# Last attention of a twelve-stage network: the first pass over a sequence taken in two halves, the preparation of its rows in two parts

## The reference

```python
def _L3_attn_ref(x, ln_g, ln_b, Wq, bq, Wk, bk, Wv, bv):
    H = 16
    xn = (x - mu) * jax.lax.rsqrt(var + EPS) * ln_g + ln_b
    q = (xn @ Wq + bq).reshape(B, T, H, D // H)      # k and v likewise
    scale = 1.0 / math.sqrt(D // H)
    attn = jnp.einsum('bnhd,bmhd->bnmh', q, k) * scale
    w = jax.nn.softmax(attn, axis=2)
    y = jnp.einsum('bnmh,bmhd->bnhd', w, v).reshape(B, T, D)
    return y
```

## Time and profile before

| what | value |
|---|---|
| median of three runs | 2432.96 us (2432.85 to 2443.46) |
| the profiled execution | 2443.27 us |
| its span, first to last instruction | 2441.4 us |
| mean granted TensorE clock | 0.865 |
| TensorE busy | 1996.0 us (82%) |
| VectorE busy | 1398.0 us (57%) |
| ScalarE busy | 960.0 us (39%) |
| GpSimd busy | 139.1 us (6%) |
| the stage of the change | about 2064 to 2345 us of the span |

### The profile page before, as it was taken

One profiled execution on the slowest core, in us unless ns is written; L12 is line 12 of the kernel. 1 busy time (PEld: TensorE's weight loads), 2 busy tenths in 40 slices (PEclk: granted clock), 3 DMA queues, 4 the chain that ended last, 5 costly groups with the idle time before them and its releaser, 6 DMA issues. The chain is left out here.

```text
span 2441.4 us, 38225 instructions
## 1 busy us (share of the span) xinstructions
PE 1996.0 (82%) x13180; PEld 1561.6 (64%) x13180; DVE 1398.0 (57%) x3614; ACT 960.0 (39%) x2141; POOL 139.1 (6%) x195
## 2 busy tenths in 40 slices
PE   3588778669967884997999899999799975888775
PEld 2355455358953223997999678787699963555543
DVE  6645455666668997666222256667522247555547
ACT  1345444332223321223444355555344444333344
POOL 1100000110001002000000000000000000000000
PEclk9779788769989995998999999999899987666668
DMA  5000000000000001000000044444100000000000
GB/s 139 31 1 1 1 1 1 31 16 1 0 1 0 1 0 50 1 0 1 1 0 0 20 136 130 129 134 129 32 1 0 0 0 0 1 1 0 0 1 17
DMA packets 47459, 61.63 MB, mean 25 GB/s; under 512 B 7126, under 2 KB 44726, under 8 KB 46744
## 3 DMA queue, kind: packets, MB, share of 16 engines
q1 hardware_dynamic: 47356, 60.31, 8.0%
HBM read 34.08 MB, written 26.21 MB: 25 GB/s over the span
## 5 line engine op out<-in xcount | busy, mean ns | idle before, releaser
L760 ACT ACTIVATE m2a_hid<-psum,m_b 128x256 f32<-128x256 f32 x256 | 100.5, 475 | 114.6 <-PE psum L55 114.5
L760 ACT ACTIVATE m2b_hid<-psum,m_b 128x256 f32<-128x256 f32 x256 | 100.5, 475 | 114.2 <-PE psum L55 114.2
L745 PE MATMUL psum<-m_w,m2a_hid 128*128 128x128 f32 x1024 | 126.2, 277 | 0.0
L745 PE MATMUL psum<-m_w,m2b_hid 128*128 128x128 f32 x1024 | 126.2, 277 | 0.0
L778 DVE SCALAR_TENSOR_TENSOR m2a_acc<-psum,m2a_gates,m2a_acc 128x128 f32<-128x128 f32 x128 | 39.0, 347 | 148.4 <-PE psum L745 148.4
L778 DVE SCALAR_TENSOR_TENSOR m2b_acc<-psum,m2b_gates,m2b_acc 128x128 f32<-128x128 f32 x128 | 39.0, 347 | 148.1 <-PE psum L745 148.1
L745 PEld LDWEIGHTS psum<-m_w,m2a_hid 128*128 128x128 f32 x1024 | 122.1, 194 | 0.6
L745 PEld LDWEIGHTS psum<-m_w,m2b_hid 128*128 128x128 f32 x1024 | 122.1, 194 | 0.6
L2150 ACT ACTIVATE a_p<-a_p,a_nmax 128x256 f32<-128x256 f32 x128 | 64.0, 500 | 143.0 <-DVE a_nmax L2174 143.0
L1881 DVE TENSOR_REDUCE a_nmax<-psum 128x2 f32<-128x512 f32 x128 | 82.9, 687 | 49.5 <-PE psum L1722 49.4
L1115 DVE TENSOR_TENSOR_SCAN a1s_clamped<-a1s_clamp_coef,a1s_bounds 128x1024 f32<-128x1024 f32 x48 | 108.7, 2267 | 0.0
(11 more groups left out here) (625 smaller groups left out, 5509.4 us busy)
## 6 DMA issues: line engine op xcount, KB each, us to landing
a_scratch<-a_pos SPq DMA_DIRECT2D x64, 384.0 KB, 2.7
a_shifted<-a_scratch SPq DMA_DIRECT2D x64, 256.0 KB, 3.1
m_w<-in_m_w SPq DMA_DIRECT2D x1, 2048.0 KB
arena<-in_m_w SPq DMA_DIRECT2D x1, 2048.0 KB, 10.4
arena<-in_m_up SPq DMA_DIRECT2D x1, 1792.0 KB, 7.0
arena<-in_m_pick SPq DMA_DIRECT2D x2, 896.0 KB, 4.5
a_w<-in_a_w SPq DMA_DIRECT2D x1, 1536.0 KB, 7.8
out<-X SPq DMA_DIRECT2D x1, 1024.0 KB, 5.0
```

Source lines behind the costliest of these rows:

```text
L745: last = nc.tensor.matmul(ps_y(e % 2)[:, t * D:(t + 1) * D], hid[:, e % 2, c * SEQ + t * P:c * SEQ + (t + 1) * P], m.m2_w2[:, e, c, :], st ...
L760: last = nc.scalar.activation(hid[:, e % 2, c * SEQ:(c + 1) * SEQ], ps_up(e % 2)[:, c * SEQ:(c + 1) * SEQ], ACT.Gelu, bias=m.m2_b1[:, e * ...
```

## The change

The stack `st` gets a second buffer, chosen by `u`. The taking of the rows (`start_c`, now the one addition) and their splitting (`start_e`, new) are parted, with a new semaphore `rows_taken` between the addition and the second shifted turn, which writes the same bank. `turn_stack` becomes `turn_keys` (rounds 0 and 1) and `turn_queries` (rounds 2 and 3 and v). In a unit heads 8 to 15 of the sequence's own first pass stand among score groups 1 to 3, and heads 0 to 7 of the next sequence's among groups 5 to 7; the second shift stands ahead of group 4. The norm's beginning is taken two units ahead, so all engines use `threaded_two_ahead`: units 0, then a loop of two rounds over the units 1 and 2, then units 5, 6 and 7 written out. ScalarE's `unit` keeps its calls, with `move_shifted(u, n, 1)` behind group 3 and `move_values(u, n, 1)` ahead of group 5.

```diff
-        st = sbr("st", [P, PAIR, 2, HEADS, 4 * HD])
+        st = sbr("st", [P, 2, PAIR, 2, HEADS, 4 * HD])
...
             def start_a(u, n):                       # TensorE
                 if not isinstance(n, int) or n:
-                    pe.wait_ge(shift_moved, 2 * n)
+                    pe.wait_ge(shift_moved, 2 * n - 1)
...
+            def turn_queries(u, n):
+                if not isinstance(n, int) or n:
+                    pe.wait_ge(shift_moved, 2 * n)
+                turn_heads(ps_stack(2), u, 0, 0).then_inc(turned, 1)
+                pe.wait_ge(moved, 4 * n + 1)
+                turn_heads(ps_stack(3), u, 0, 1).then_inc(turned, 1)
                 pe.wait_ge(moved, 4 * n + 2)
...
+            def turn_shifted(u, n, half, next_rows):
                 pe.wait_ge(shift_ready, 2 * n + half + 1)
+                if next_rows:
+                    pe.wait_ge(rows_taken, n + 2)
+                turn_heads(ps_x, u, 0, half).then_inc(shift_turned, 1)
...
-                for h in range(HEADS):
+                for h in range(8):
                     plain_scores(0, 0, h)
+                turn_shifted(0, 0, 0, False)
                 scores(0, 0, 0)
...
+            def unit(u, n, prev, next, next2):       # TensorE
+                scores(u, n, 1)
+                if prev:
+                    values(1 - u, n - 1, 3)
+                if next:
+                    start_a(1 - u, n + 1)
+                for h in (8, 9):
+                    plain_scores(u, n, h)
+                if next:
+                    start_b(1 - u, n + 1)
+                for h in (10, 11):
+                    plain_scores(u, n, h)
+                scores(u, n, 2)
+                if prev:
+                    turn_back(1 - u, n - 1, 3)
+                for h in (12, 13):
+                    plain_scores(u, n, h)
+                scores(u, n, 3)
+                for h in (14, 15):
+                    plain_scores(u, n, h)
+                values(u, n, 0)
+                turn_shifted(u, n, 1, next)
+                turn_back(u, n, 0)
+                scores(u, n, 4)
+                if next:
+                    turn_keys(1 - u, n + 1)
+                    turn_queries(1 - u, n + 1)
+                scores(u, n, 5)
+                values(u, n, 1)
+                if next:
+                    for h in range(4):
+                        plain_scores(1 - u, n + 1, h)
+                scores(u, n, 6)
+                turn_back(u, n, 1)
+                if next:
+                    for h in range(4, 8):
+                        plain_scores(1 - u, n + 1, h)
+                scores(u, n, 7)
+                values(u, n, 2)
+                if next:
+                    turn_shifted(1 - u, n + 1, 0, False)
+                turn_back(u, n, 2)
+                if next:
+                    scores(1 - u, n + 1, 0)
...
+            def unit(u, n, prev, next, next2):       # VectorE
+                if next:
+                    start_b(1 - u, n + 1)
+                for h in range(8, 12):
+                    maxima(u, n, h)
+                if next:
+                    start_c(1 - u, n + 1)
+                if prev:
+                    normalise(1 - u, n - 1, 3)
+                for h in range(12, 16):
+                    maxima(u, n, h)
+                shift(u, n, 1)
+                if next:
+                    start_e(1 - u, n + 1)
+                if prev:
+                    end_a(1 - u, n - 1)
+                normalise(u, n, 0)
+                if next:
+                    start_d(1 - u, n + 1)
+                    for h in range(4):
+                        maxima(1 - u, n + 1, h)
+                if prev:
+                    end_b(1 - u, n - 1)
+                normalise(u, n, 1)
+                if next:
+                    for h in range(4, 8):
+                        maxima(1 - u, n + 1, h)
+                    shift(1 - u, n + 1, 0)
+                if next2:
+                    start_a(u, n + 2)
+                normalise(u, n, 2)
...
-            threaded(dve, first, unit, tail)
+            threaded_two_ahead(dve, first, unit, tail)
```

More of the change, by code:

```diff
@@ L1692, in start_b, with turn_heads @@
                 last.then_inc(qk_ready, 1)
-            def turn_heads(out, a, half):
+            def turn_heads(out, u, a, half):
                 for j in range(2):
@@ L1697, in turn_heads, with turn_keys @@
                         heads = slice(8 * half + 4 * j, 8 * half + 4 * j + 4)
-                        last = nc.tensor.transpose(out[:, j, t * P:(t + 1) * P], st[:, t, a, heads, :].rearrange("p h f -> p (h f)").bitcast(F32),
+                        last = nc.tensor.transpose(out[:, j, t * P:(t + 1) * P], st[:, u, t, a, heads, :].rearrange("p h f -> p (h f)").bitcast(F32),
                                                    m.ident[:, :])
                 return last
-            def turn_stack(u, n):
+            def turn_keys(u, n):
                 pe.wait_ge(st_ready, n + 1)
[L1704 to L1707, removed]
+                for r in range(2):
+                    turn_heads(ps_stack(r), u, 1, r).then_inc(turned, 1)
+            def turn_queries(u, n):
[4 more added lines that the diff above has]
+                turn_heads(ps_stack(3), u, 0, 1).then_inc(turned, 1)
                 pe.wait_ge(moved, 4 * n + 2)
@@ L1761, in first @@
                 start_b(0, 0)
-                turn_stack(0, 0)
-                for h in range(HEADS):
+                turn_keys(0, 0)
+                turn_queries(0, 0)
+                for h in range(8):
                     plain_scores(0, 0, h)
-                turn_shifted(0, 0, 0)
+                turn_shifted(0, 0, 0, False)
                 scores(0, 0, 0)
[L1768 to L1794, removed]
@@ L1798, in tail @@
                 turn_back(u, n, 3)
-            threaded(pe, first, unit, tail)
+            threaded_two_ahead(pe, first, unit, tail)
         @block.scalar
@@ L1807, in start_b, with move_stack @@
                 nc.scalar.activation(xT[:, :], ps_x[:, 0, :], ACT.Identity, bias=m.a3_ln_b[:, 0:1], scale=m.a3_ln_g[:, 0:1]).then_inc(xT_ready, 1)
-            def move_stack(u, n):
-                for r in range(4):
+            def move_stack(u, n, turns):
+                for r in turns:
                     act.wait_ge(turned, 4 * n + r + 1)
@@ L1829, in first @@
                 start_b(0, 0)
-                move_stack(0, 0)
+                move_stack(0, 0, range(4))
                 move_shifted(0, 0, 0)
[L1833 to L1848, removed]
+            def unit(u, n, prev, next, next2):
+                exps(n, 0)
+                if prev:
+                    move_values(1 - u, n - 1, 3)
+                if next:
+                    start_b(1 - u, n + 1)
+                exps(n, 1)
+                exps(n, 2)
+                exps(n, 3)
+                move_values(u, n, 0)
+                move_shifted(u, n, 1)
+                exps(n, 4)
+                if next:
+                    move_stack(1 - u, n + 1, range(4))
+                move_values(u, n, 1)
+                exps(n, 5)
+                exps(n, 6)
+                exps(n, 7)
+                move_values(u, n, 2)
+                if next:
+                    move_shifted(1 - u, n + 1, 0)
+            threaded_two_ahead(act, first, unit, lambda u, n: move_values(u, n, 3))
         @block.vector
@@ L1886, in shift @@
                 low = nmax[:, heads, :].rearrange("p h t -> p t h")
[L1887 removed]
+                nc.vector.tensor_copy(st[:, u, :, 0, heads, 3 * HD], low)
                 nc.vector.drain()
[L1889 removed]
+                nc.vector.tensor_tensor(st[:, u, :, 0, heads, 3 * HD + 1], low, st[:, u, :, 0, heads, 3 * HD].bitcast(F32), ALU.subtract).then_inc(shift_ready, 1)
             def normalise(u, n, j):
@@ L1916, in first @@
                 start_b(0, 0)
+                start_a(1, 1)
                 start_c(0, 0)
+                start_e(0, 0)
                 start_d(0, 0)
-                for h in range(HEADS):
+                for h in range(8):
                     maxima(0, 0, h)
[L1921 to L1949, removed]
```

34 lines of the change are left out of this document (22 added, 12 removed).

## The result

The changed kernel takes 2415.13 us (median of four runs, 2411.7 to 2418.23) against 2436.99 us of the kernel before on the same chip: ratio 0.9897, 95% interval 0.9876 to 0.9918. It is faster, by 21.9 us of medians where 14.2 were forecast. Its profiled execution took 2418.23 us, 25.0 less than that of the kernel before.

The account below looks back on a forecast made before the run. No engine is full; TensorE and VectorE waiting for each other, and the clock, set a period. Periods -13.3, start -4.4 and last unit +3.5 sum to -14.2 us, from median 2432.96 to 2418.8; range 2406 to 2435.

Parts of the forecast that it names:

- start: Stage up to its first scores: first shifted turn 5.0 us earlier, second stack's memsets +0.6, together -4.4 us.
- periods: Seven stretches from one unit's first scores to the next's: each from 32.04 to 30.14 us, together -13.3 us.
- last unit: Unit after the seven periods: gets eight more products and maxima at low clock, forecast +3.5 us.
- the walk of a unit: New unit's TensorE queue priced step by step: 33.92 us at low clock, 30.7 with 6.8 us high, 29.7 with 10.2.
- high clock, 8.7 us taken: 2.4 GHz time per unit, taken from the earlier trace; rise put mid-stack at 16.8 us, giving 30.14 us a unit.
- VectorE's wait for plain products: VectorE's waits over the seven periods, 47.4 us: to fall from 6.8 a unit to about 4, in short pieces.
- The single waits of the walk: TensorE's waits within a new unit: 0.86 before product 14, 1.36 and 1.67 in next-sequence products, 0.45 before scores 4.
- Rival B: Clock stays low through the units: 33.92 us each, +12.3 us in all, 2445 us; chance 0.09.
- C: Clock rises a second time in a unit, among values 2 to values 3: 27.9 us each, 2403 us; chance 0.08.
- D: High clock is kept, VectorE's chain and the moves bound: 25.2 us a unit, 2384 us; chance 0.02.
- The rule of the Trainium skill: TensorE's clock does not drop without long idle gaps between matmul bursts; by it the new unit would keep 2.4 GHz.
- A: No change: products 10 to 15 wait for maxima at full pair price, 1.7 us a unit lost, 2431 us; chance 0.21.

## Why the prediction was right, and where its terms were wrong

Direction held: start, periods and last unit were taken apart rightly, the walk of a unit held, and the time lies in the range. Three terms were mis-sized, and together the stage lost 25.3 us where the sum has 14.2. That the median still came out only 3.7 us from the forecast of 2418.8 is partly luck: the median before that it was counted from, 2432.96, rose by 4.0 with a fourth run.

The periods: -13.3 forecast, 7 x (29.30 - 32.04) = -19.2 measured. The walk itself was near: the six full units took 29.58 on the mean with 10.2 us of high clock, where it has 29.7. Two things make up most of the 5.9. The walk of a full unit was counted seven times, but the first of the seven has no sequence before it to finish; it took 27.6 where 30.14 was counted, 2.5 less. And high clock, 8.7 us taken, was 10.2 in the other six units (9.8 with the first), which is 30.14 less 29.7 six times, 2.6. One price was wrong without showing in the total: each score group was priced at 0.73 and added, but groups 0 and 1, which use different rows, take 0.73 together (2205.24 to 2205.97); the row at 2094.05 in the earlier trace rows, eight products in 0.81, shows as much. In the unit above, scores 4 so began at 14.80 where the walk has 15.27, but what follows took longer than in the walk, and the unit had 30.9 with 6.8 us of high clock where the walk has 30.7.

The start: -4.4 forecast, -3.5 measured to the first exponential. The changed kernel had the low clock throughout its start (0.50 above); the kernel before 0.56.

The last unit: +3.5 forecast, -2.5 measured. The step that failed is that it would stay at the low clock as before. It had 13.7 us of high clock. The price of the eight moved products was right: the kernel with the normalisations early, whose last unit has not got them, took 19.3 with the same 13.7 us, 3.4 less. The clock outweighed it; the same last unit had taken 25.2 without high clock. The prediction had read the rises off the unit in the earlier trace rows, where q and k and the stack stand before them. But the rise at 2290.86 in the kernel before came ahead of both (2292.08 and 2297.44), and the changed kernel's last unit, which has neither, rose at 2295.47 and at 2305.71.

Of the reasons, one failed. The prediction let VectorE's wait for plain products fall from 6.8 a unit to about 4, as if the spread of the pairs brought the gain. It fell to 43.0 / 7 = 6.1, and TensorE's waits for maxima did not fall at all (18.6 and 18.4). What went is the wait of values for a normalisation behind maxima and a shift, 1.42 at a time, a line that the prediction named but did not price by itself; the kernel before with only that mended has 10.9 of the 19.2 us of the periods and 19.4 of the 23.5 of whole times, in part by more high clock, and the changed kernel with only that undone loses 7.6 us of stage. The halves with the split preparation bring the rest in the trace (8.4 us of stage; by medians 4.1, with intervals that overlap), and without the split it is lost.

The single waits of the walk were near: 0.86 for product 14 (0.72 on the mean of eight units), 0.99 and 1.30 for products 2 and 6, which is 1.36 and 1.67 less the 0.37 of the next product (0.78 and 0.87 in the seven units), 0.45 for the scores behind the shifted turn (0.34), none for the second shifted turn (none).

Rival B (low clock throughout) did not occur: the clock rose 11 to 18 us after a unit's first exponential in the seven units. C occurred in part: twice in the seven units a second rise came, at 2176.0 and 2268.2, and the units at 15.5 and 17.1 us of high clock took 28.5 and 27.6 us against 29.9 to 31.2 at 6.8, the first unit aside. D did not: with no wait of TensorE over 1.1 us, the clock fell in every unit, as in the kernel before. The rule of the Trainium skill cited with it (TensorE: Matmul & The Clock Gate, Why this matters for your kernels) did not hold for this stage. The longest wait before was misread, though: it is not 1.5 us but 2.28, ahead of the stack at 2297.44. A did not occur either.

## What to carry to other kernels

Before dividing a pass, look at what stands behind it in the in-order queue: a half-microsecond normalisation behind four maxima held up products for 1.4 us, and moving the normalisations gave most of what the whole rearrangement gave (19.4 of 23.5 us). When a pass is spread over a queue, part what others wait for from what merely follows (here 0.7 us of taking rows from 1.8 us of preparing them), or the spread brings nothing. Price neighbouring products that use different rows together where a row shows them so (here 0.73 for two groups), not one by one. And walk the first and the last unit of a pipeline by themselves, for they lack a part of the others.

## What the runs showed of the hardware

A unit's time hangs on its share of high clock, by about 0.3 us a microsecond: in the changed kernel 31.2 us at 6.8 and 27.6 at 17.1. The last unit of the kernel before took 25.2 us without high clock and 19.3, by the same instructions, with 13.7 us of it. Idle full-size transposes put into waits raised the mean clock of the periods from 0.67 to 0.71 and shortened them in one trace; with the same time filled with products of 32 rows one trace had 0.67 and 29.33 us, while the clocks of whole executions (0.875 to 0.882 and 0.871 to 0.886) do not tell the two apart. Equal code ahead of the stage differed by up to 16 us between profiled executions, more than most of the edits moved, so that the stage in the trace told more than the whole time.
